# Leaving out the filler products in the first step of a recurrent attention and mixture-of-experts kernel on one Trainium2 core

## The chip, the core and the metric

The kernel runs on one core of a Trainium2 chip. A core has five engines with queues of their own: TensorE (PE in the profile, its weight loads PEld), VectorE (DVE), ScalarE (ACT), GpSimd (POOL) and SyncE (SP), which starts the transfers. Each executes its instructions in order and waits on semaphores that the others raise. The metric is the device time of the whole launch in microseconds (us).

## The reference, cut to what matters

The input x is (2, 2048, 256), 32-bit floats. It is normalised over its last axis and goes through two branches whose product is added back:

```
xn = layernorm(x)
dx = shift_by_one_token(xn) - xn
xm = xn + dx * x_miu
mix = tanh(xm @ x_A)                       # six groups of 32
miu = lambdas + mix[g] @ x_B[g]            # for r, w, k, v, a, g
r_in, w_in, k_in, v_in, a_in, g_in = xn + dx * miu
v = v_in @ vW.T;  r = r_in @ rW.T;  g = tanh(g_in @ g_A) @ g_B
w = -softplus(-(w_miu + tanh(w_in @ w_A) @ w_B)) - 0.5
k = normalised(k_in @ kW.T + tanh(k_in @ k_A) @ k_B)
a_gate = 2 * sigmoid(a_time + a_in @ a_A @ a_B)
y = wkv7(r, w, kk, v, -k, k * a_gate)      # recurrence over tokens, state 64x64 a head
s = (group_norm(y) + bonus) * g @ oW.T
f = sum over 8 experts of gate * (relu(xn @ wi.T + bi + lora_e) @ wo.T + bo)   # top 2
out = x + s * silu(f)
```

## The kernel before, in words

The 2048 tokens of both sequences are cut into 16 tiles of 2 x 64 tokens a sequence. A pipeline of three stages runs over them in 18 steps: "front" (norm, mixing, projections) of tile s in step s, "rec" (the recurrence and the experts) in step s + 1, "post" (the output product) in step s + 2. Step 1 holds a front alone. Each engine has a program written out by hand, in which the stages of a step are interleaved; inside an engine the order is fixed, and between engines semaphores set it.

In step 1 TensorE has little to do and waits often. Its order there is xt_ (four transposes of xn), route, mix (the product with x_A), miu(0), miu(1), kW, wk_A, g_A, wk_B, a_A, miu(2), a_B, norm, r_, v_, g_B, xmt_, bonus_, diag. What it waits for:

- route waits for ScalarE's xnc (the copy of the transposed xn out of PSUM, L911).
- mix waits for VectorE's xm (L1384).
- miu(0) waits for ScalarE's mixt, the tanh of mix's result (L919, L920), and for the second group of weight loads, of which w_kW is the last. ScalarE works on mixt after the exponentials of the expert gate (exps, L941 and L942).
- miu(1) waits for VectorE to have used miu(0)'s result (mtmp, L1394); GpSimd then adds xnc to it and makes xd (L1195), which kW, wk_A and the other projections read.
- r_ waits for the fifth xd; bonus_ for VectorE's dg (L1460).

Between these stand calls of warm, which multiplies one zeroed 128x128 block (the second xnc buffer, not yet used) with a zeroed 128x256 one into the bank FB; nobody reads the result. A call is two instructions on the chip, all with the line L297:

```
def warm(n):
    for _ in range(n):
        mm(FB[:, 0:256], xnc[1][:, 0, 0:128], xnc[1][:, 1, :], start=True, stop=True)
```

Step 1 has 21 calls: 5 before xt_, then 1, 2, 4 and 4 up to miu(1), 2 after norm and 3 after xmt_. The products of mm2, which most projections use, stand at L253 (in two halves of 64 columns) or L254 (whole).

Of the kernel before, what the change touches and what calls it, by code (L numbers as in the profile page):

```python
# [66 lines left out]
def program(nc, x, par, weights, consts, out):  # L67
    ctx = ExitStack()
    with ctx:
# [24 lines left out]
        def till(name, n):  # L94

            return S(name), at(name) + n
# [123 lines left out]
        def wait_loaded(engine, i):  # L220

            engine.wait_ge(loaded_by[i], 16 * (len(GROUPS[i]) + (i == 0)))
# [23 lines left out]
        def _(pe):  # L246
# [47 lines left out]
# [4 lines that stand above are left out]
# [19 lines left out]
            def xt_():  # L317
                pe.wait_ge(*till("xn_done", G))
                if not steps["front"]:
                    wait_loaded(pe, 0)  # L320
                to_channels(used_by("xt"), xn, "xt_mm")

            def route(half=False):
                pe.wait_ge(*till("xnc_done", 1))
                for g in range(G):
                    for c in range(2):
                        last = mm2(half, used_by("route")[:, g * 136:(g + 1) * 136], xnc[steps["front"] % 2][:, c, g * L:(g + 1) * L],
                                  w["route"][:, c, :], start=(c == 0), stop=(c == 1))
                last.then_inc(S("route_mm"), 1)

            def mix(half=False):
                pe.wait_ge(*till("xm_done", 2))
                for u in range(2):
                    for c in range(2):
                        last = mm2(half, used_by("mix")[:, u * 256:(u + 1) * 256], w["x_A"][:, c, u * 128:(u + 1) * 128], xm[:, c, :],
                                  start=(c == 0), stop=(c == 1))
                last.then_inc(S("mix_mm"), 1)

            def miu(pair):
                pe.wait_ge(*till("mixt_done", 2))  # L340
                for c in range(2):
                    for k in (2 * pair, 2 * pair + 1):
                        q = MIX_ORDER[k]
                        o, u = 32 * (q % 4), q // 4
                        last = mm(MIU[k % 2][:, c * 256:(c + 1) * 256],  # L345
                                  w["x_B"][o:o + 32, u, c * 128:(c + 1) * 128], mixt[o:o + 32, u, :], start=True, stop=True)
                last.then_inc(S("miu_mm"), 1)
# [7 lines left out]
            def wk_A():  # L355
                pe.wait_ge(*till(f"xd_{SLOT[W_]}_done", 1))
                pe.wait_ge(*till(f"xd_{SLOT[K_]}_done", 1))
                for c in range(2):
                    for o, name, q in ((0, "w_A", W_), (64, "k_A", K_)):
                        last = mm(used_by("wk_A")[o:o + 64, 0:G * L], w[name][:, c, :], xd[:, q, c, :], start=(c == 0), stop=(c == 1))  # L360
                last.then_inc(S("wk_A_mm"), 1)

            def a_A():
                pe.wait_ge(*till(f"xd_{SLOT[A_]}_done", 1))
                for c in range(2):
                    last = mm(used_by("a_A")[64 * c:64 * c + 64, 0:G * L], w["a_A"][:, c, :], xd[:, A_, c, :], start=True, stop=True)
                last.then_inc(S("a_A_mm"), 1)

            def g_A(half=False):
                low("g_A", G_, 128, half)  # L370

            def wk_B():
                pe.wait_ge(*till("hwk_done", 1))
                for c in range(2):
                    for o in (0, 64):
                        mm(used_by("wk_B")[o:o + 64, c * 256:(c + 1) * 256], w["wk_B"][0:64, c * 128 + o:c * 128 + o + 64],  # L376
                           h_wk[0:64, :], start=True, stop=True)
                        last = mm(used_by("kW")[o:o + 64, c * 256:(c + 1) * 256], w["wk_B"][64:128, c * 128 + o:c * 128 + o + 64],
                                  h_wk[64:128, :], start=False, stop=True, skip_group_check=True)
                last.then_inc(S("wk_B_mm"), 1)  # L380

            def a_B(half=False):
                pe.wait_ge(*till("ha_done", 1))
                for c in range(2):
                    last = mm2(half, used_by("a_B")[:, c * 256:(c + 1) * 256], w["a_B"][:, c * 128:(c + 1) * 128], h_a[:],
                              start=True, stop=True)
                last.then_inc(S("a_B_mm"), 1)

            def kW(half=False):
                pe.wait_ge(*till(f"xd_{SLOT[K_]}_done", 1))  # L390
                for c in range(2):
                    for k in range(2):
                        mm2(half, used_by("kW")[:, c * 256:(c + 1) * 256], w["kW"][:, k, c * 128:(c + 1) * 128], xd[:, K_, k, :],
                           start=(c == 0 and k == 0), stop=False, skip_group_check=True)

            def r_(half=False):
                pe.wait_ge(*till(f"xd_{SLOT[R_]}_done", 1))
                for c in range(2):
                    for k in range(2):
                        last = mm2(half, used_by("r")[:, c * 256:(c + 1) * 256], w["rW"][:, k, c * 128:(c + 1) * 128],  # L400
                                  xd[:, R_, k, :], start=(k == 0), stop=(k == 1))
                last.then_inc(S("r_mm"), 1)

            def v_(half=False):
                pe.wait_ge(*till(f"xd_{SLOT[V_]}_done", 1))
                for g in range(G):
                    for k in range(2):
                        last = mm2(half, used_by("v")[:, g * C:(g + 1) * C], xd[:, V_, k, g * L:(g + 1) * L], w["vW"][:, k, :],
                                  start=(k == 0), stop=(k == 1))
                last.then_inc(S("v_mm"), 1)  # L410
# [8 lines left out]
            def norm(half=False):  # L419
                pe.wait_ge(*till("ksum_done", 1))  # L420
                mm2(half, used_by("norm")[:, 0:G * L], ones[:], ksum[:], start=True, stop=True).then_inc(S("nrm_mm"), 1)
# [180 lines left out]
            def tile(step, front, rec, post):  # L602
# [13 lines left out]
                if step == 1:  # L616
                    if front:
                        xt_()
                        warm(1)
                        route()  # L620
                        warm(2)
                        mix()
                        warm(4)
                        if step == 1:
                            wait_loaded(pe, 1)
                        miu(0)
                        warm(4)
                        pe.wait_ge(*till("mx_0_done", 2))
                        pe.wait_ge(*till("mx_1_done", 2))
                        miu(1)  # L630
                        kW(half=True)
                        wk_A()
                        wait_loaded(pe, 2)
                        pe.wait_ge(*till("xnc_done", 1))
                        g_A(half=True)
                        pe.wait_ge(*till("route_read", 1))
                        wk_B()
                        pe.wait_ge(*till("mixt_done", 2))
                        a_A()
                        pe.wait_ge(*till("mx_2_done", 2))  # L640
                        pe.wait_ge(*till("mx_3_done", 2))
                        miu(2)
                        pe.wait_ge(*till("kraw_done", 1))
                        pe.wait_ge(*till("ksq_done", 1))
                        a_B()
                        pe.wait_ge(*till("hwk_done", 1))
                        norm()
                        warm(2)
                        pe.wait_ge(*till("hg_done", 1))
                        r_()  # L650
                        pe.wait_ge(*till("sig_done", 2))
                        v_()
                        pe.wait_ge(*till("ha_done", 1))
                        g_B()
                        pe.wait_ge(*till("agate_done", 2))
                        xmt_()
                        warm(3)
                        pe.wait_ge(*till("nrm_done", 1))
                        bonus_()
                        pe.wait_ge(*till("r_done", 1))  # L660
                        pe.wait_ge(*till("gate_done", 1))
                        diag(rec)
# [1230 lines left out]
```

## Time and profile before

| | us |
|---|---|
| median of 3 runs | 1017.18 |
| lowest and highest | 1015.92, 1017.49 |
| the profiled execution, as timed | 1017.24 |
| its span, first to last instruction | 1015.4 |
| TensorE busy | 997.9 |
| VectorE busy | 842.5 |
| ScalarE busy | 660.5 |

The profile shows one execution, in microseconds from its first instruction; what lies around the span is not in it. L297 is line 297 of the kernel. Matmuls overlap in the array: the start-to-start distance is less than the duration of one, and ends are modelled. The granted clock is TensorE's share of 2.4 GHz, so 1.00 is 2.4 GHz and 0.50 is 1.2 GHz.

### The profile page before, as it was taken

The page shows a single profiled execution, that of the slowest core. Times are in us where ns is not written, and L with a number is a line of the kernel's source. Part 1 is how long each engine was busy: PE and PEld are TensorE (multiplying, and loading weights), DVE is VectorE, ACT ScalarE, POOL GpSimd, SP SyncE. Part 2 cuts the span into 40 slices and gives each one's busy share as a digit, 9 for nine tenths or more (in the row PEclk, how much of TensorE's full clock was granted, in tenths as well). Part 3 has the DMA queues.
Part 4 walks back from the last instruction along what each step waited for, and adds up shares of the span by engine and source line. Part 5 has one row for each costly group of instructions (what it writes and reads, how often), then busy time and mean ns, then how long its engine had stood idle before and what let it go on. Part 6 is the DMA issues. An engine that isn't in the chain of part 4 may idle for free.

```text
span 1015.4 us, 45487 instructions
## 1 busy us (share of the span) xinstructions
PE 997.9 (98%) x19952; PEld 783.6 (77%) x19952; DVE 842.5 (83%) x1674; ACT 660.5 (65%) x1458; POOL 457.3 (45%) x541
## 2 busy tenths in 40 slices
PE   9999999999999999999999999999999999999996
PEld 6777778777787877778777787877778777787774
DVE  5887979888888888989888888888889889798864
ACT  3656675756768576676756767576676666757563
POOL 3372534535344362543635445363543725445422
PEclk9999999999999999999999999999999999999998
DMA  7000000000000000000000000000000000000000
GB/s 251 12 4 3 3 4 23 4 23 3 12 15 4 23 4 23 3 4 23 4 24 4 3 24 3 23 4 23 3 4 23 3 23 3 3 23 5 13 4 22
DMA packets 9267, 17.13 MB, mean 17 GB/s; under 512 B 1904, under 2 KB 3824, under 8 KB 8816
## 3 DMA queue, kind: packets, MB, share of 16 engines
q1 hardware_dynamic: 9072, 14.23, 4.3%
q8 instruction: 159, 2.61, 1.0%
q14 instruction: 36, 0.29, 0.1%
HBM read 10.03 MB, written 4.19 MB: 14 GB/s over the span
## 4 chain that ended last, share of the span: by engine, by line
PE 93%; DVE 3%; issue 2%; ACT 2%; POOLq 0%; POOL 0%; DVEq 0%
PE bank L254 37%; PE bank L253 14%; PE grams L468 10%; PE bank L345 5%; PE bank L494 2%; PE grams L537 2%; PE bank L483 2%; PE bank L527 2%; PE grams L442 2%; PE bank L568 2%; PE grams L592 2%; PE grams L557 2%; PE bank L360 2%; PE bank L376 2%; PE bank L302 2%
## 5 line engine op out<-in xcount | busy, mean ns | idle before, releaser
L1214 POOL TENSOR_TENSOR bk<-bk,tot 128x256 f32<-128x256 f32 x192 | 154.4, 815 | 209.2 <-PE grams L468 209.2
L1528 DVE COPY_PREDICATED gm<-c_mask_g,grams 128x1024 f32<-128x1024 int32 x96 | 160.1, 1668 | 13.9 <-PE grams L468 13.9
L900 ACT ACTIVATE relu<-bank,prm 128x256 f32<-128x256 f32 x256 | 107.1, 470 | 83.2 <-PE bank L254 82.0
L1195 POOL TENSOR_TENSOR xd<-mtmp,xnc 128x512 f32<-128x512 f32 x96 | 120.7, 1272 | 34.4 <-DVE mtmp L1394 34.4
L254 PE MATMUL bank<-xnc,w_wi 128*128 128x256 f32 x512 | 124.5, 386 | 0.4 <-ACT relu L900 0.4
L468 PEld LDWEIGHTS grams<-ar,bk 64*64 64x64 f32 x6144 | 100.3, 134 | 23.4 <-issue 15.3
L1004 ACT ACTIVATE gl<-gm 32x128 f32<-32x128 f32 x320 | 98.8, 309 | 28.3 <-DVE gm L1528 21.6
L254 PE MATMUL bank<-xmt,w_lora_B 128*128 128x256 f32 x444 | 114.5, 387 | 0.0
L468 PE MATMUL grams<-ar,bk 64*64 64x64 f32 x6144 | 111.4, 220 | 2.5 <-ACT scratch L1182 2.0
L254 PEld LDWEIGHTS bank<-xnc,w_wi 128*128 128x128 f32 x512 | 94.4, 190 | 18.3 <-issue 5.6
L1538 DVE TENSOR_TENSOR ar<-ar,tot 128x512 f32<-128x512 f32 x96 | 93.0, 968 | 17.5 <-PE grams L468 17.3
L1394 DVE SCALAR_TENSOR_TENSOR mtmp<-bank,prm,dx 128x256 f32<-128x256 f32 x192 | 80.2, 473 | 22.0 <-PE bank L345 22.0
L1245 POOL TENSOR_TENSOR bk<-kh,rootd 128x512 f32<-128x512 f32 x16 | 28.2, 1763 | 153.2 <-PE bank L527 150.0
L254 PEld LDWEIGHTS bank<-xmt,w_lora_B 128*128 128x128 f32 x444 | 80.5, 190 | 15.1 <-issue 5.0
L253 PE MATMUL bank<-w_wo,hid 128*64 128x256 f32 x768 | 90.9, 379 | 0.0
L253 PEld LDWEIGHTS bank<-w_wo,hid 128*64 128x64 f32 x768 | 52.6, 137 | 23.3
L1226 POOL TENSOR_TENSOR out_t<-out_t,x_in 128x512 f32<-128x512 f32 x16 | 20.3, 1268 | 77.0 <-DVE out_t L1517 77.0
L345 PE MATMUL bank<-mixt,w_x_B 32*128 32x256 f32 x384 | 54.3, 400 | 0.0
L1496 DVE TENSOR_TENSOR hid<-relu 128x512 f32<-128x512 f32 x64 | 48.4, 776 | 0.6
L911 ACT ACTIVATE xnc<-bank 128x512 f32<-128x512 f32 x15 | 9.0, 597 | 49.5 <-PE bank L302 49.5
L1577 DVE TENSOR_TENSOR state<-dec,bank 128x256 f32<-128x256 f32 x32 | 13.3, 417 | 33.2 <-PE bank L578 33.2
L1203 POOL TENSOR_TENSOR tot<-tot 128x256 f32<-128x256 f32 (+2 forms) x96 | 39.5, 412 | 2.7
(207 smaller groups left out, 2227.0 us busy)
## 6 DMA issues: line engine op xcount, KB each, us to landing
x_in<-x SPq DMA_DIRECT2D x16, 256.0 KB, 2.8
out<-out_t SPq DMA_DIRECT2D x16, 256.0 KB, 2.0
w_wi<-w_wi_dram SPq DMA_DIRECT2D x1, 1024.0 KB, 7.0
w_wo<-w_wo_dram SPq DMA_DIRECT2D x1, 1024.0 KB, 9.4
w_lora_B<-w_lora_B_dram SPq DMA_DIRECT2D x1, 512.0 KB, 8.8
w_x_A<-w_x_A_dram SPq DMA_DIRECT2D x1, 256.0 KB, 2.6
w_x_B<-w_x_B_dram SPq DMA_DIRECT2D x1, 256.0 KB, 2.6
w_kW<-w_kW_dram SPq DMA_DIRECT2D x1, 256.0 KB, 3.5
```

The lines of the kernel that those rows point to most:

```text
L253: last = mm(out[o:o + 64, :], lhsT[:, o:o + 64], rhs, **kw)
L254: return last if half else mm(out, lhsT, rhs, **kw)
L345: last = mm(MIU[k % 2][:, c * 256:(c + 1) * 256], w["x_B"][o:o + 32, u, c * 128:(c + 1) * 128], mixt[o:o + 32, u, :], start=True, stop=True)
L468: last = mm(dst, bk[o:o + 64, g, c, 1 - b, k, :], rhs, start=True, stop=True)
L900: A(dst[:, p % 2, j * 256:(j + 1) * 256], ZB[p % 2][:, j * 256:(j + 1) * 256], ACT.Relu, bias=prm[:, P_BI + 2 * p + j:P_BI + 2 * p + j + 1 ...
L1004: A(gl[l % 2][o:o + 32, :, :, :].rearrange("p q g (c n m) -> p (q g c) n m", c=2, m=m), right(gm[o:o + 32, :, :, :, b, 0, 32 * k:32 * k + ...
L1195: tt(xd[:, q, :, :], mtmp[:, k % 2, :, :], xnc[steps["front"] % 2][:, :, :], ALU.add).then_inc(S(f"xd_{k}_done"), 1)
L1214: tt(v, v, d, ALU.mult).then_inc(S(f"bk{k}_scaled"), 1)
L1394: run(v.scalar_tensor_tensor(mtmp[:, k % 2, c, :], MIU[k % 2][:, c * 256:(c + 1) * 256], prm[:, P_LAM + 2 * q + c:P_LAM + 2 * q + c + 1], ...
L1496: run(v.tensor_tensor(hid[:, p, :], relu1[:, p % 2, :], relu2[:, p % 2, :], ALU.add), f"hid_{p}_done")
L1528: run(v.copy_predicated(dst, msk.to_broadcast([128, 32, HALF // m, m]), src), "g_stored")
L1538: run(v.tensor_tensor(a, a, tv[:, :, 0].unsqueeze(1).unsqueeze(3).to_broadcast([128, 2, 4 * n, m]), ALU.mult), "ar_scaled")
```

## The change

Sixteen of the 21 calls of warm are left out: the 1, 2, 4 and 4 between xt_ and miu(1), the 2 after norm and the 3 after xmt_. The five before xt_ stay. No other instruction, wait or transfer is added, moved or taken away.

```
                     if front:
                         xt_()
-                        warm(1)
                         route()
-                        warm(2)
                         mix()
-                        warm(4)
                         if step == 1:
                             wait_loaded(pe, 1)
                         miu(0)
-                        warm(4)
                         pe.wait_ge(*till("mx_0_done", 2))
                         pe.wait_ge(*till("mx_1_done", 2))
                         miu(1)
...
                         norm()
-                        warm(2)
                         pe.wait_ge(*till("hg_done", 1))
                         r_()
...
                         xmt_()
-                        warm(3)
                         pe.wait_ge(*till("nrm_done", 1))
                         bonus_()
```

## Rows read from the trace of the kernel before

**Rows 1.** The page, the chain that ended last: shares by engine.

```profile
PE 93%; DVE 3%; issue 2%; ACT 2%; POOLq 0%; POOL 0%; DVEq 0%
```

**Rows 2.** Timeline of TensorE, 0 to 18 us: start, duration, instructions, [idle before].

```profile
1.99 4.63 PE L297 MATMUL bank<-xnc 128*128 128x256 f32 x10 [1.99 <-DVE scratch L1786]
...
7.50 0.66 PE L297 MATMUL bank<-xnc 128*128 128x256 f32 x2
8.39 1.19 PE L254 MATMUL bank<-w_route,xnc 128*128 128x136 f32 x8 [0.24 <-ACT xnc L911]
9.42 1.03 PE L297 MATMUL bank<-xnc 128*128 128x256 f32 x4
10.28 1.89 PE L254 MATMUL grams<-xm,w_x_A 128*128 128x256 f32 x8
12.01 1.89 PE L297 MATMUL bank<-xnc 128*128 128x256 f32 x8
13.83 1.13 PE L345 MATMUL bank<-mixt,w_x_B 32*128 32x256 f32 x8
14.89 1.99 PE L297 MATMUL bank<-xnc 128*128 128x256 f32 x8
16.82 1.13 PE L345 MATMUL bank<-mixt,w_x_B 32*128 32x256 f32 x8
```

**Rows 3.** Timeline of all engines, 0 to 18 us: VectorE and ScalarE.

```profile
9.24 0.88 DVE L1384 SCALAR_TENSOR_TENSOR xm<-dx,prm,xnc 128x256 f32<-128x256 f32 x2
...
11.91 0.28 ACT L942 ACTIVATE e<-top,nm 128x1 f32<-128x1 f32 x1
12.21 0.38 ACT L919 ACTIVATE mixt<-grams 128x256 f32<-128x256 f32 x1
12.49 0.36 ACT L920 ACTIVATE mixt<-grams 64x256 f32<-64x256 f32 x1
...
15.01 1.66 DVE L1394 SCALAR_TENSOR_TENSOR mtmp<-bank,prm,dx 128x256 f32<-128x256 f32 x4 [4.31 <-PE bank L345]
```

**Rows 4.** The chain that ended last, 14 to 37 us: start, length, piece.

```profile
22.65 0.60 ACT kraw L959
...
33.06 0.48 DVE dg L1460
```

**Rows 5.** Timeline of TensorE, 27 to 34 us.

```profile
27.09 1.97 PE L254 MATMUL grams<-xd,w_rW 128*128 128x256 f32 x8 [0.51 <-POOL xd L1195]
...
33.68 0.43 PE L449 MATMUL bank<-dg,c_headsel 128*32 128x128 f32 x8 [0.30 <-DVE dg L1460]
```

**Rows 6.** Single lines: durations in ns (min/median/max), first and last start.

```profile
L297 PE MATMUL bank<-xnc x6: 631/631/792, 2.0 to 4.3; 128*128 128x256 f32 x6
...
L297 PE MATMUL bank<-xnc x42: 379/379/792, 2.0 to 33.0; 128*128 128x256 f32 x42
...
L302 PE MATMUL grams<-c_ident,xn x4: 421/421/444, 6.6 to 7.3; 128*128 128x128 f32 x4
...
L302 PE MATMUL bank<-c_ident,xn x4: 272/272/273, 42.0 to 42.4; 128*128 128x128 f32 x4
```

**Rows 7.** Windows: length, TensorE busy (instructions), granted clock, DMA share, GB/s.

```profile
954.80:956.80 2.00, 0.00 (x0) 1.00 0.00 0
...
1001.25:1004.25 3.00, 0.00 (x1) 1.00 0.21 81
1004.25:1004.75 0.50, 0.00 (x0) 0.55 0.00 0
1007.20:1010.90 3.70, 3.67 (x16) 0.50 0.00 0
...
1011.00:1011.25 0.25, 0.00 (x0) 0.75 0.00 0
```

**Rows 8.** A weight load: its issue in the timeline, and KB and us to landing.

```profile
6.38 0.44 SPq L1800 DMA_DIRECT2D w_kW<-w_kW_dram x1
...
w_kW<-w_kW_dram SPq DMA_DIRECT2D x1, 256.0 KB, 3.5
```

More of the change, by code:

```diff
@@ L618, in tile @@
                         xt_()
-                        warm(1)
                         route()
-                        warm(2)
                         mix()
-                        warm(4)
                         if step == 1:
@@ L626, in tile @@
                         miu(0)
-                        warm(4)
                         pe.wait_ge(*till("mx_0_done", 2))
@@ L647, in tile @@
                         norm()
-                        warm(2)
                         pe.wait_ge(*till("hg_done", 1))
@@ L656, in tile @@
                         xmt_()
-                        warm(3)
                         pe.wait_ge(*till("nrm_done", 1))
```

## The prediction

> **What bounds the kernel now.** I read the page first: TensorE carries 93% of the chain that ended last [rows 1]. So whatever delays TensorE in the first step delays the end by as much, unless another engine was the later one at that place. The change touches only the first 35 us, so I read the timeline of TensorE there [rows 2], beside it what ScalarE and VectorE did when TensorE waited [rows 3], then the chain for the places where it leaves TensorE [rows 4], the two late groups of fillers [rows 5], the durations that tell the clock at the start [rows 6], the windows in which the granted clock fell and rose later [rows 7], and a weight load [rows 8].
>
> The reader is to see three things. First, TensorE looks busy from 1.99 to 25 us, but the rows L297 are fillers: products of a zeroed buffer that nobody reads. Second, behind each group of fillers stands a real group that waits for another engine, so a filler costs something only where it ends later than that engine. Third, the first five fillers (10 instructions) ran at half the later speed.
>
> **The unit.** One call of warm is two matmul instructions (10 for warm(5) in [rows 2]). At the full clock the eight instructions of mix take 1.89 us [rows 2], the last of them 0.38 to its modelled end, as the median product of this width does [rows 6]: (1.89 - 0.38)/7 = 0.216 us from start to start, so 0.43 us a call. The change removes 16 calls, 32 instructions: 32 x 0.216 = 6.9 us of TensorE's time. Nearly all of it lies in waits.
>
> **The change, group by group.**
>
> - warm(1) at 7.50: two instructions, gone by about 8.0. route starts at 8.39, released by ScalarE's xnc, with 0.24 us idle before it [rows 2]. Worth 0.
> - warm(2) at 9.42: four instructions, 9.42 + 0.86 = 10.28, where mix starts. VectorE's xm ends at 9.24 + 0.88 = 10.12 [rows 3]. How long TensorE takes from a release to its start I read at two places where it had run out of work: miu(1) starts at 16.82 after VectorE's 15.01 + 1.66 = 16.67, 0.15 later [rows 2, 3]; bonus starts at 33.68 after 33.06 + 0.48 = 33.54, 0.14 later [rows 4, 5]. By 0.15 mix would start at 10.27. Even with no delay at all (10.12) it wins nothing: the product goes to ScalarE's mixt, which starts at 12.21 behind the last exponential, ended at 11.91 + 0.28 = 12.19 [rows 3]. Worth 0.
> - warm(4) at 12.01: eight instructions, 12.01 + 1.73 = 13.74; miu(0) starts at 13.83. What miu(0) needs, mixt, is ready at 12.49 + 0.36 = 12.85 [rows 3]. The last of the loads that it waits for, w_kW, was issued at 6.38 and took 3.5 [rows 8], so it is in by 9.9 to 10.3 and does not hold it. Without fillers it starts at 12.85 + 0.15 = 13.00: **0.83 us earlier**. The bounds are 0.98 (no delay from the release) and 0.6 (the 0.36 that the last ScalarE instruction itself takes as a delay, as a pessimistic one). This is the one group on the path.
> - warm(4) at 14.89: 14.89 + 1.73 = 16.62, and VectorE, which miu(1) waits for, ends at 16.67 [rows 2, 3]. The two end together: 0 to 0.10 to gain; I take 0.05.
> - warm(2) before r_: r_ starts at 27.09 after 0.51 us in which TensorE idled for GpSimd's xd, fillers done [rows 5]. Worth 0, with 0.5 us of slack.
> - warm(3) before bonus: bonus starts at 33.68, after 0.30 us idle for VectorE's dg, which ends at 33.54 [rows 4, 5]. Worth 0, 0.3 us of slack.
>
> **Does the 0.88 reach the end?** Up to 22.6 us the chain is TensorE alone: miu(1), kW, wk_A, g_A, wk_B follow each other, and wk_B's end releases ScalarE's kraw at 22.65 [rows 4]. Each input of these (xd from GpSimd) descends from miu(0) and moves with it. From 22.65 to 33.54 the chain is ScalarE and VectorE (two table loads, square root, reciprocal, kh, dg), again from wk_B's end, so it moves too; bonus and diag follow it and step 2 follows them with no pause. Nothing with a time of its own stands in between: the weight loads that step 1 waits for landed before they were wanted, and no engine gets another instruction or wait. So the sum is 0.83 + 0.05 = 0.88, about **0.9 us**, against 1017.24 us for the profiled execution (span 1015.4 and 1.8 around it): **1016.3**. The median of the three runs shown, 1017.18, is the same time, but the three spread over 1.6 us.
>
> **The clock, which can take it back.** The granted clock is the only other thing the fillers touch. The windows call it 1.00 from time 0, but durations say otherwise: the first fillers took 631 ns against 379 ns later, and the transposes at 6.6 to 7.3 took 421 ns against 272 ns at 42 us [rows 6]. So TensorE was at 1.2 GHz until about 7.5 us, after 5.6 us of work, and at 2.4 GHz for route. The five fillers that stay, and the transposes behind them, are what ran before the rise; the first removed filler begins only at 7.50.
>
> After the change TensorE pauses four times: about 0.5 us before route, 0.8 before mix, 0.9 before miu(0) (12.1 to 13.0), 1.8 before miu(1) (14.1 to 15.9), then works densely to 25; later some 1.5 us each before r_ and before bonus. Later in the trace a single pause of 2.0 us at 954.80 left the clock at 1.00; one from 1001.25 had let it fall in the window 1004.25 to 1004.75, after 3.0 us or more; and it came back in 1011.00 to 1011.25, just after 3.7 us of dense work at 0.50 [rows 7]. Every pause of the changed kernel is shorter than the one that did no harm. But no row shows several with only 1.1 us of work between two of them, as here around miu(0), and clock changes need not meet the program at the same place in each execution.
>
> The price if it falls: dense work of 3.7 to 3.9 us at half speed before it rises, as at 1007.2, is work that takes half as long at the full clock: a loss of **1.9 us** per fall. Where the work at half speed has slack behind it, less.
>
> The Trainium skill (TensorE: Matmul & The Clock Gate, section "A second HAM failure mode: psum-queue depth-cycling") says that frequent short idles between groups of matmuls can make the clock swing between its levels. That rule speaks against this change; the trace neither bears it out nor excludes it, for before the change it has no such row of pauses. By it the result would be the second or third rival below rather than the forecast.
>
> **Rivals.**
>
> 1. *Nothing comes of it.* Another release turns out as late as the filler (a delay of 0.9 us at miu(0)). Against it: 0.15 and 0.14 measured at two such places. Time: 1017.2.
> 2. *The clock falls once*, in the pauses around miu(0) (12.1 to 15.9), and miu(1), kW and wk_A run at half speed until it returns. For it: two pauses close together, 2.7 us idle out of 3.8. Against it: the 2.0 us pause that did nothing. Time: 1016.3 + 1.9 = 1018.2. With a second fall before bonus, so that step 2 begins slow: 1020.1.
> 3. *The five fillers alone don't carry the clock up* and it stays low through the thin stretch. Extra, doubling what is on the path: route's issue doubles and ends near 10.3, mix then takes 7 x 0.43 + 0.63 = 3.6 us to 13.9, mixt's two instructions 0.64 (12.21 to 12.85) and the release 0.15, so miu(0) is late by 14.7 - 13.0 = 1.7 us; if work at half speed raises the clock there, it ends at 1016.3 + 1.7 = 1018.0. If it holds on through both miu (2 x 0.9) and the first 3.8 us of the dense stretch (1.9), the sum is 1016.3 + 1.7 + 1.8 + 1.9 = **1021.7**. This is the one that ends on the other side. It decides as soon as the slow work costs 2.9 us (0.9 given back and 2.0 on top), that is once miu(1) too runs slow. For it: the rise came only at about 7.5, at the edge of what stays. Against it: at half speed route and mix close up by themselves to over 5 us of nearly unbroken work, more than preceded the rise at 1011.
>
> **How the numbers follow.** A run of this kernel tells no change from one below 0.2%, about 2.0 us. Forecast (clock stays, 0.9 us gained): 0.58, at 1016.3. Rival 1: 0.07. Rival 2 with one fall: 0.16, at 1018.2. Rival 3 with an early rise: 0.05, at 1018.0. These four are all within 0.2%, 0.86 less some 0.04 for noise in either direction: 0.82. Slower: rival 3 in full (0.08), two falls (0.04), and 0.02 of that noise: 0.14. Faster: the other 0.02 of the noise and 0.02 for what I have not seen, 0.04; the terms found sum to 0.9 us, and even their upper bounds (0.98 + 0.10) to 1.1. The low end of the range is the fastest run shown less the gain, 1015.92 - 0.9 = 1015.0; the high end, 1019.2, is one fall (1018.2) and 1.0 more for the spread of the runs. It leaves out two falls and rival 3 in full.
>
> **What would show it.** miu(0) at 13.0 instead of 13.83, mixt unmoved at 12.21; miu(1) at 15.9 to 16.0; kraw at 21.8; bonus at 32.8; 379 ns for every 256-column product after 8.4 us, and idle time before miu(1) of some 1.8 us. A kW or miu(1) product of some 630 ns means rival 2; route products of twice 279 ns mean rival 3. The prediction is wrong if the clock falls for more than one short stretch, or if step 2 does not move with bonus.

## The result and the profile after

The changed kernel takes 1020.48 us (median of 13 runs, 1018.49 to 1022.82), the kernel before 1017.18 (13 runs, 1015.92 to 1018.58). The ratio is 1.003, with a 95% interval from 1.0022 to 1.0039: **slower by 3.3 us**, where 0.9 us faster was forecast and 1019.2 was the top of the range. The granted clock says where to look. Its mean over a run is 0.989 to 0.993 in the 13 runs of the changed kernel (median 0.991), and 0.993 to 0.998 in the 86 runs of the kernel before that stand beside the experiments below (median 0.996); only five of these 86 have 0.993.

The profiled execution of the changed kernel is its shortest: 1018.49 us, span 1016.7. This is its timeline of TensorE in the first step, to be held against [rows 2, 5]; line numbers of VectorE and ScalarE are 6 lower than before.

```profile
6.34 0.63 PE L302 MATMUL grams<-c_ident,xn 128*128 128x128 f32 x4 [0.29 <-DMA c_eye<-c_eye_dram]
7.66 1.19 PE L254 MATMUL bank<-w_route,xnc 128*128 128x136 f32 x8 [0.69 <-ACT xnc L905]
9.44 1.99 PE L254 MATMUL grams<-xm,w_x_A 128*128 128x256 f32 x8 [0.59 <-DVE xm L1378]
12.26 1.13 PE L345 MATMUL bank<-mixt,w_x_B 32*128 32x256 f32 x8 [0.83 <-ACT mixt L914]
15.15 1.70 PE L345 MATMUL bank<-mixt,w_x_B 32*128 32x256 f32 x8 [1.75 <-DVE mtmp L1388]
16.78 3.02 PE L253 MATMUL bank<-xd,w_kW 128*64 128x256 f32 x16
...
26.61 1.96 PE L254 MATMUL grams<-xd,w_rW 128*128 128x256 f32 x8 [0.92 <-POOL xd L1189]
...
33.64 0.42 PE L449 MATMUL bank<-dg,c_headsel 128*32 128x128 f32 x8 [2.04 <-DVE dg L1454]
```

What ends the waits before miu(0) and miu(1), from the timelines of ScalarE and VectorE:

```profile
11.75 0.36 ACT L914 ACTIVATE mixt<-grams 64x256 f32<-64x256 f32 x1
```

```profile
13.43 1.66 DVE L1388 SCALAR_TENSOR_TENSOR mtmp<-bank,prm,dx 128x256 f32<-128x256 f32 x4 [3.46 <-PE bank L345]
```

The forecast gain is there. Before, miu(0) started 13.83 - 12.85 = 0.98 us after mixt was ready; now it starts 12.26 - 12.11 = 0.15 after, so 0.83 us are won, exactly the term of the sum. Before miu(1) the distance fell from 0.15 to 15.15 - 15.09 = 0.06, 0.09 won where 0.05 was put. Together 0.92.

(That mixt itself is ready 0.74 us earlier than before is no effect of the change, for the transposes stand ahead of all that was left out. They began 0.28 us earlier (6.34 against 6.62) and took 0.63 in place of 1.08 us, at the full clock already, as they did too when the kernel before was run again.)

Then the loss. miu(1) takes 1.70 us where it took 1.13, and the 16 halves of kW take 3.02 us where they took 1.95. kW in the kernel before:

```profile
17.88 1.95 PE L253 MATMUL bank<-xd,w_kW 128*64 128x256 f32 x16
```

The windows of the profile after (length, busy time of PE, PEld, DVE, ACT, POOL, granted clock, DMA share, GB/s):

```profile
12.00:15.00 3.00, 1.13 (x8) 0.76 (x8) 1.57 (x4) 0.11 (x1) 0.61 (x1) 1.00 1.01 300
15.00:16.00 1.00, 0.85 (x6) 0.75 (x8) 0.09 (x1) 0.00 (x0) 1.00 (x2) 0.79 1.00 328
16.00:18.50 2.50, 2.50 (x12) 1.14 (x12) 1.61 (x5) 0.00 (x0) 1.52 (x2) 0.50 1.00 395
18.50:19.50 1.00, 1.00 (x10) 0.62 (x8) 0.90 (x5) 0.00 (x0) 1.00 (x2) 0.76 1.09 457
...
958.00:961.00 3.00, 3.00 (x18) 2.34 (x12) 2.71 (x2) 0.00 (x0) 2.59 (x5) 0.50 0.00 0
```

The clock falls between 15 and 16 us, just as miu(1) begins, and is back between 18.5 and 19.5. From mixt to bonus it is 33.64 - 12.11 = 21.53 us, before 33.68 - 12.85 = 20.83. So 0.70 slower although 0.92 were won: this fall cost 1.6 us. A second stretch at half speed lies at 958, behind the pause before step 17, which the change does not touch; the kernel before kept 1.00 there, up to 1004 us. What it costs shows further below, where the time is taken apart.

### The profile page after: what moved, and what is told of

Same layout as the page of the kernel before. It is cut to its first block, busy times and chain, and to the rows that moved or that the text cites. A ratio compares the mean times of both kernels' runs of the same rounds, so it can differ in the third digit from the quotient of the medians.

```text
span 1016.7 us, 45423 instructions
## 1 busy us (share of the span) xinstructions
PE 993.4 (98%) x19920; PEld 779.3 (77%) x19920; DVE 842.0 (83%) x1674; ACT 660.4 (65%) x1458; POOL 456.9 (45%) x541
## 4 chain that ended last, share of the span: by engine, by line
PE 89%; DVE 6%; issue 2%; ACT 2%; SPq 0%; DMA 0%; POOLq 0%; POOL 0%; DVEq 0%
PE bank L254 36%; PE bank L253 13%; PE grams L468 10%; PE bank L345 5%; PE grams L537 2%; PE bank L494 2%; PE bank L483 2%; PE bank L527 2%; PE grams L442 2%; PE bank L568 2%; PE grams L592 2%; PE grams L557 2%; PE bank L360 2%; PE bank L376 2%; DVE gm L1522 2%
```

## The experiments

Each median below is to be held against the kernel before, run in turn with it on the same chip: 1017.15 us for the first four (35 runs), 1017.05 for the others (22 and 29 runs on two other chips). Only the fillers differ between these kernels; none changes what is computed for the output.

**The kernel before, again** (no edit).

> The kernel before, unchanged, to see the mean granted clock of its runs beside their times. If the difference is the clock, its runs have 0.995 to 0.996 (one stretch at the end at half speed, and the last 3 us) against 0.989 to 0.993 for the changed kernel, and the time is 1017.2. If the changed kernel loses elsewhere, its clocks are as low as those of the changed kernel.

1016.96 us, ratio 0.9998 (0.999 to 1.0007), clocks 0.995 to 0.998. Its profile holds 1.00 from the rise to the pause of the last step:

```profile
6.60:1003.00 996.40, 987.45 (x19923) 777.28 (x19922) 837.86 (x1655) 656.00 (x1450) 451.88 (x528) 1.00 0.05 16
```

So the lower clocks belong to the change.

**The early groups back, the late ones out.**

```
                         xt_()
+                        warm(1)
                         route()
+                        warm(2)
                         mix()
+                        warm(4)
...
                         miu(0)
+                        warm(4)
```

> The changed kernel with the four groups up to miu(1) (1, 2, 4 and 4 calls) back, the two late groups (2 and 3) still out. Theory A (the clock falls in the pauses around miu(0) and miu(1), or does not rise before them): 1017.0 to 1017.5, clock 0.995. Theory B (the clock falls in the two late pauses, before r_ and bonus, and step 2 begins slow): 1019.5 to 1020.5, as the changed kernel. If both pauses count: between, 1018 to 1019.

1018.26 us, ratio 1.0009 (0.9999 to 1.0018): 1.1 us over the kernel before, 2.2 under the changed one. Its runs have clocks of 0.993 to 0.998. The interval of the ratio just includes no loss at all, but it ends below that of the changed kernel, which begins at 1.0022: putting the early groups back helps, and they are the larger part. By the medians it is the case between, in which both pauses count.

**The late groups back, the early ones out.**

```
                         norm()
+                        warm(2)
...
                         xmt_()
+                        warm(3)
```

> The changed kernel with the two late groups (2 calls after norm, 3 after xmt_) back, the four early ones out. Theory A: still 1020 to 1020.5. Theory B: 1016.3, with the 0.9 us that the early groups give back. Both: 1018 to 1019.

1019.30 us, ratio 1.0021 (1.0012 to 1.0029): 2.15 over the kernel before, 1.2 under the changed one. The two parts add up by the medians, 1.1 + 2.15 = 3.25 against 3.3, though the 1.2 won here lies within the noise (the changed kernel's interval is 1.0022 to 1.0039). Theory B would have given 1016.3 and has fallen as the sole cause. The profile has the fall at 15 to 16 us again, and none behind the late pause:

```profile
15.00:16.00 1.00, 0.74 (x6) 0.64 (x8) 0.20 (x1) 0.00 (x0) 1.00 (x2) 0.84 1.08 369
16.00:18.80 2.80, 2.80 (x16) 1.39 (x14) 1.75 (x6) 0.00 (x0) 1.81 (x2) 0.50 1.03 415
...
33.00:40.00 7.00, 6.02 (x152) 4.99 (x152) 5.06 (x14) 2.90 (x8) 0.85 (x3) 1.00 0.01 2
```

**Only the group between miu(0) and miu(1) back.**

```
                         miu(0)
+                        warm(4)
```

> The changed kernel with only the group between miu(0) and miu(1) (4 calls) back. Theory A in the form that the 1.8 us pause before miu(1) makes the clock fall: if it is the only cause, 1016.3 and a clock of 0.995. Theory C (the five first fillers alone often leave the clock low, and it rises late): little better than the changed kernel, 1019 to 1020. Theory B: no better than the changed kernel.

1019.25 us, ratio 1.0019 (1.001 to 1.0028). I had expected 1016.3 if that pause was the only cause. The time would fit theory C, but the profile does not: the clock was up before route, as in all the others. In its profile it does cure the fall at 15 us; the first fall now comes behind the late pause, where this kernel has no filler:

```profile
14.00:18.00 4.00, 4.00 (x30) 2.68 (x30) 2.66 (x8) 0.00 (x0) 2.99 (x3) 1.00 0.94 352
30.00:33.00 3.00, 1.18 (x19) 0.69 (x21) 2.90 (x5) 2.71 (x6) 1.60 (x2) 1.00 0.00 0
33.40:34.00 0.60, 0.60 (x42) 0.60 (x35) 0.28 (x2) 0.24 (x2) 0.00 (x0) 0.63 0.00 0
34.00:36.80 2.80, 2.80 (x21) 2.23 (x14) 2.19 (x6) 0.20 (x1) 0.19 (x1) 0.50 0.02 6
```

**The changed kernel, a second and a third profile** (no edit).

> The changed kernel, unchanged, for a second profile of it. By the mean clocks of its 13 runs (0.989 to 0.993) the theory of the clock expects four or five stretches of 3.4 us at half speed, against two in the kernel before: one or more in the first 20 us, where TensorE pauses before miu(0) and miu(1), perhaps one at 33 to 40 us behind the pause before bonus, the two at the end. If the loss is elsewhere, 1.00 from 6 to 1000 us and a step longer than 61.35.

> The changed kernel unchanged, for a third profile. The theory of the clock expects a stretch at half speed that begins at 15 to 16 us, behind the pause before miu(1), as in both profiles of it so far, and the time to follow the number of such stretches: 1.7 us for each over the two of the kernel before, less 0.9.

1023.93 and 1020.52 us, one execution each; the first is longer than all 13 runs above. The second profile shows all the places at once. Its windows:

```profile
15.00:16.00 1.00, 0.68 (x4) 0.60 (x6) 0.27 (x1) 0.00 (x0) 1.00 (x2) 0.69 0.93 336
16.00:22.00 6.00, 6.00 (x30) 3.23 (x28) 4.34 (x14) 0.00 (x0) 3.53 (x3) 0.50 1.01 400
22.00:23.00 1.00, 1.00 (x11) 0.65 (x8) 0.83 (x6) 0.38 (x1) 0.00 (x0) 0.89 1.06 323
...
35.40:36.40 1.00, 0.67 (x17) 0.46 (x20) 1.00 (x2) 0.98 (x3) 0.00 (x0) 0.73 0.00 0
36.40:39.20 2.80, 2.80 (x67) 2.50 (x64) 1.55 (x4) 0.06 (x1) 0.00 (x0) 0.50 0.00 0
```

Here the clock stays low twice as long after miu(1), and falls again as step 2 begins. In its timelines mixt is ready at 12.29 and bonus starts at 35.49: 23.20 us, against 20.83 before, so 2.4 more, or 3.3 for the fall with the 0.92 won taken out. The mark that ScalarE leaves at the end of step 2 tells what the second fall costs, and the one at the end of step 16, which releases TensorE into step 17, what comes later. In the order before, after, second and third profile of the changed kernel, each from its own timeline:

```profile
97.05 0.20 ACT L1182 ACTIVATE scratch<-eps 128x1 f32<-128x1 f32 x1
...
956.55 0.19 ACT L1182 ACTIVATE scratch<-eps 128x1 f32<-128x1 f32 x1
```

```profile
97.02 0.20 ACT L1176 ACTIVATE scratch<-eps 128x1 f32<-128x1 f32 x1
...
956.61 0.20 ACT L1176 ACTIVATE scratch<-eps 128x1 f32<-128x1 f32 x1
```

```profile
100.24 0.20 ACT L1176 ACTIVATE scratch<-eps 128x1 f32<-128x1 f32 x1
...
960.54 0.19 ACT L1176 ACTIVATE scratch<-eps 128x1 f32<-128x1 f32 x1
```

```profile
98.87 0.20 ACT L1176 ACTIVATE scratch<-eps 128x1 f32<-128x1 f32 x1
...
958.79 0.19 ACT L1176 ACTIVATE scratch<-eps 128x1 f32<-128x1 f32 x1
```

With mixt ready at 12.85, 12.11, 12.29 and 12.50, bonus at 33.68, 33.64, 35.49 and 34.08, and the ends of the spans, each execution falls into four parts:

| us | before | after | second | third |
|---|---|---|---|---|
| mixt ready to bonus | 20.83 | 21.53 | 23.20 | 21.58 |
| to the end of step 2 | 63.37 | 63.38 | 64.75 | 64.79 |
| to the end of step 16 | 859.50 | 859.59 | 860.30 | 859.92 |
| to the end of the span | 58.85 | 60.09 | 61.56 | 59.91 |

The two executions whose clock fell at 34 to 36 lose 1.4 us in the second part, the other none. In the last part all three lose 1.1 to 2.7 us, and all three have a stretch at half speed as step 17 begins, which the kernel before has not. In the profile after, that is nearly the whole difference of the two spans: 1016.7 - 1015.4 = 1.3 us, of which 1.24 arise there.

In the third profile the first fall comes after 17 us, not at 15 to 16 as I had expected, and takes part of kW and wk_A instead of miu(1); and its time is not 1.7 us for each stretch less 0.9. Its stretches at 17, 34 and 959 us would give 5.1 - 0.9 = 4.2 over the kernel before; it has 3.5, for the second and the third cost less (1.42 and 1.06 in the table).

**Fillers of 16 columns.** The kernel before with all its calls, but narrow ones after the first five. This tells array work from the mere presence of the instructions.

```
-mm(FB[:, 0:256], xnc[1][:, 0, 0:128], xnc[1][:, 1, :], ...)
+mm(FB[:, 0:256 if n == 5 else 16], xnc[1][:, 0, 0:128],
+   xnc[1][:, 1, 0:256 if n == 5 else 16], ...)
```

> The kernel before, with the 16 later fillers still there as instructions, but 16 columns wide in place of 256, so that they take almost no time in the array; the first five are left as they were. Theory A (what the fillers give is array work that holds the clock up): as the changed kernel, 1019.5 to 1020.5, mean clock 0.991 to 0.993. Rival (their instructions or order matter, such as the weight loads or the place where TensorE stands at its waits): as the kernel before, 1017.2 and 0.996.

1019.11 us, ratio 1.0023 (1.0011 to 1.0035), clocks 0.989 to 0.994: 0.4 under the range expected for theory A, but its interval overlaps that of the changed kernel and lies clear of the kernel before. The fillers between miu(0) and miu(1) are there, and miu(1) runs slow all the same:

```profile
13.56 1.07 PE L297 MATMUL bank<-xnc 128*128 128x16 f32 x8
15.38 1.89 PE L345 MATMUL bank<-mixt,w_x_B 32*128 32x256 f32 x8 [0.76 <-DVE mtmp L1394]
```

**Fillers fitted to the waits.**

```
 xt_(); warm(1); route(); warm(2); mix()
-warm(4)
+warm(2)
 miu(0); warm(4); ...
 norm()
-warm(2)
+warm(3)
 ...; xmt_(); warm(3); bonus_()
```

> Fillers fitted to the waits: 1, 2, then 2 calls in place of 4 before miu(0) (they end at 12.87, when mixt is ready), 4 before miu(1), 3 in place of 2 before r_, 3 before bonus. The theory of two separate terms (0.8 us of delay at miu(0), the rest clock) expects the 0.8 us without the loss: 1016.3, mean clock 0.996 as before. If every gain in step 1 ends in a longer wait for VectorE: 1017.1.

1016.94 us, ratio 0.9993 (0.9984 to 1.0002), clocks 0.994 to 0.998. In its profile mixt is ready at 12.02 + 0.36 = 12.38 and miu(0) starts at 12.53, 0.15 later, as in the changed kernel, with no fall until the end. The time is 0.1 us under that of the kernel before by the medians and 0.7 by the ratio; the interval holds both no gain and all of the expected 0.8.

**Three groups, only for the long pauses.**

```
                         miu(0)
+                        warm(4)
...
                         norm()
+                        warm(3)
...
                         xmt_()
+                        warm(3)
```

> The changed kernel with three groups back: 4 calls between miu(0) and miu(1), 3 before r_, 3 before bonus; nothing between the transposes and miu(0). If the three long pauses (1.8, 1.0 and 2.0 us) are what lets the clock fall: 1016.3 to 1017, mean clock 0.996. If the short pauses before route, mix and miu(0) count too: 1018 to 1019.

1016.84 us, ratio 0.9996 (0.9987 to 1.0004). It lies in the range expected for the three long pauses. The fillers between the transposes and miu(0) are not needed: their pauses may stay if the long ones are filled.

**Fillers in the last steps too.** f1, and calls before step 17, before the last transposes and before the output product, the last two into a bank whose reader is done (warm takes the bank as a second argument for that).

```
                         v_()
+                        if step == TILES:
+                            pe.wait_ge(*till("y1_read", 1)); warm(4)
...
                         rec_inc(1)              # end of step 17
+                        pe.wait_ge(*till("relu2_3_done", 2)); warm(7, ZB[1])
...
                         zt_()
+                        if step == TILES + 2: warm(3, ZB[1])
```

> f1, and fillers in the pauses of the last steps: 4 calls in the 2.0 us before step 17, 7 in the 3.5 us before the last transposes, 3 before the output product. If the clock is what these pauses cost, the stretch at half speed at 1004 to 1011 disappears: transposes 1.08 to 0.60, output product 3.68 to 1.90 us, so 2.2 us less than f1, and 0.5 more on average from the pause before step 17: 1013.6, mean clock 0.999 or more. Rival (the end hangs on VectorE, ScalarE and the store, not on TensorE): no change against f1.

1014.42 us, ratio 0.9972 (0.9962 to 0.9983): 2.6 us under the kernel before, the fastest version of the study. The end of its timeline, and below it that of f1:

```profile
1000.80 3.29 PE L297 MATMUL bank<-xnc 128*128 128x256 f32 x14
1004.40 0.63 PE L302 MATMUL bank<-c_ident,zz 128*128 128x128 f32 x4 [0.31 <-DVE scratch L1787]
1004.87 1.46 PE L297 MATMUL bank<-xnc 128*128 128x256 f32 x6
1006.85 1.95 PE L253 MATMUL bank<-w_oW,zt 128*64 128x256 f32 x16 [0.52 <-ACT zt L995]
```

```profile
1003.87 1.08 PE L302 MATMUL bank<-c_ident,zz 128*128 128x128 f32 x4 [3.53 <-DVE scratch L1780]
1006.31 3.60 PE L253 MATMUL bank<-w_oW,zt 128*64 128x256 f32 x16 [1.36 <-ACT zt L988]
```

The output product takes 1.95 instead of 3.60 us: 1.65 us at the end of the path. The transposes take 0.63 instead of 1.08, but that gives nothing. The output product waits for ScalarE's zt, and zt stands behind a table load and ysg, here in f1:

```profile
1003.85 1.28 ACT L992 ACT_TABLE_LOAD   x1
1005.14 0.63 ACT L992 ACTIVATE ysg<-y 128x512 f32<-128x512 f32 x1
1005.68 0.58 ACT L988 ACTIVATE zt<-bank 128x512 f32<-128x512 f32 x1
```

So the output product starts 2.45 us after the transposes start (1006.85 - 1004.40), where it was 2.44. I had counted both terms, and f2 ends 0.8 us above the expected 1013.6. The medians of f1 and f2 differ by 2.5 us. The other 0.9 may be what falls before step 17 cost in some runs of f1, but the two profiles can't show it: the clock fell there in neither.

**The changed kernel with those end fillers, and with the one before step 17 alone** (the edits of f2 on the changed kernel, all three and the first only).

> The changed kernel (early and late groups of step 1 out) with the fillers of f2 in the last steps: 4 before step 17, 7 before the last transposes, 3 before the output product. If the change costs its 3.3 us only in and behind step 1 (theory A and B together), it is as far above f2 (1014.4) as the changed kernel above the kernel before: 1017.7, mean clock 0.995 to 0.997. If part of the loss arises in the pauses of the last steps, because the early change moves them against the clock: less, 1016 to 1016.5.

> The changed kernel with only the 4 calls before step 17. The clock fell behind that pause in all five profiles of kernels without the early or the late fillers (957 to 961 us) and in none of three with them. If that is more than chance and part of the 3.3 us, this wins 1.2 to 1.7 us against the changed kernel: 1018.8 to 1019.3. If it falls there in every kernel equally often, it wins about 0.5: 1020.

All three: 1017.45 us, ratio 1.001 (1.0 to 1.002), 3.0 above f2. f2 has the early start of miu(0) too, so this is to be held against the distance of the changed kernel from f1, 1020.48 - 1016.94 = 3.5: most of the loss stands when the end is covered, as expected if it arises in steps 1 and 2.

Its twelve runs also show how the time follows the clock. With a mean of 0.998 they take 1015.7 to 1016.3 us (three runs, among them the profiled one, whose only stretch at half speed is that at 15 us), with 0.996 or 0.997 1017.3 to 1018.7 (five), with 0.995 1019.2 to 1020.9 (four); the seven of f2 have 0.999 to 1.000 and take 1013.7 to 1015.2. By the windows of the profile after, a stretch at 15 to 19 us takes 0.21 + 1.25 + 0.24 = 1.7 us of granted clock, 0.0017 of the mean. So, as an estimate, these runs had one, two and three such stretches, at 1.5 to 2.3 us each by the means of the groups, and the typical run had two.

The filler before step 17 alone: 1018.85 us, ratio 1.0026 (1.0015 to 1.0036), against 1.003 (1.0022 to 1.0039) without it. The medians favour a gain of 1.6 us; the intervals overlap, so it stays undecided.

**All profiles together.** These counts go by the granted clock of the 14 profiles. Where the pauses around miu(0) and miu(1) had no full-width filler, the clock fell between 15 and 17.2 us in seven profiles of seven (the changed kernel three times, e2, e5, g1, g2). Where at least the one before miu(1) was filled, it fell there in none of seven. Behind the late pause it fell in four of eight profiles without wide fillers (a1, a2, e3, e5) and in none of six with them. Behind the pause before step 17, where that has no filler, it fell in seven of eleven: in the changed kernel's three, e2, e3, e5 and j1, not in the kernel before (twice), e1 and f1. From the end of step 16 to the last product of step 17 (L578) it is 45.1 to 46.8 us in these seven and 43.7 to 44.4 in the four, 1.6 more on average. The seven are just the profiles without full-width fillers between the transposes and miu(0), the four those with them. But the mean clocks of the runs do not bear that out: those of j1 (0.993 to 0.996, median 0.996) are no lower than those of f1 (0.994 to 0.998, median 0.995).

## Why the prediction was wrong

- *Which filler delays anything*: right. Only the one before miu(0) did, 0.83 us by forecast and by the profile; with miu(1) 0.92 against 0.88.
- *That this moves on to the end*: the chain moved with miu(0) as described up to the point where the clock fell. By itself the gain can't be told from the noise in the kernels that keep the clock (f1, j1).
- *The clock stays*: **this step failed.** It rested on "Every pause of the changed kernel is shorter than the one that did no harm". The single pause of 2.0 us was no measure for 0.8 and 1.8 us with 1.1 us of miu(0) between them: six falls in six profiles with these pauses bare, and one in one with the narrow fillers in them. Nor was it safe itself, since the clock falls behind just that pause in seven of eleven executions; one profile that had kept it was taken for a rule. The rival of one fall (1018.2) was described at its place, with a chance of 0.16, and that of two (1020.1), next to which the median of 1020.48 came out, with 0.04. Together they should have had nearly all.
- *The price of a fall*, put at 1.9 us: 1.6 in the profile after, 3.3 in the second profile, where the clock stayed low twice as long, 1.4 for the late one, 1.2 for the one behind step 17 in the profile after. The size was about right; what was missing was that it may stay down longer, and that several places fall in one execution.
- *The late pauses*, taken as some 1.5 us each: right where the clock had held up to there (1.38 before r_ and 1.58 before bonus in e1 and e3). In the changed kernel, behind the slow stretch, they are 0.92 and 2.04. The late groups, which I priced at nothing, cost 1.1 us by e1's median when left out, with an interval that reaches down to nothing.
- *Rival 3*, the five fillers alone don't carry the clock up: wrong in every profile; route ran at 279 ns in all those of the changed kernel.
- *The rule of the Trainium skill* (TensorE: Matmul & The Clock Gate, "A second HAM failure mode: psum-queue depth-cycling"), that frequent short idles between groups make the clock swing: the runs agree with it, 1.00 to 0.50 and back within 4 to 8 us, and it deserved more weight than the one row against it.
- *The sum, and what is open*: -0.9 for the early start and 3.0 for the falls in steps 1 and 2 (g1 against f2) make 2.1 us. With 1.2 for the fall behind step 17, as in the profile after, it is the 3.3 between the medians. But whether that fall comes more often because of the change is not settled: the three profiles of the changed kernel against the two of the kernel before and g2's median speak for it, while g1 against f2, and the changed kernel against f1, leave only 0.5 us for it. What decides whether the clock falls behind a given pause, when it does in four of eight or seven of eleven, no run here shows.

## What to carry to other kernels

A filler has two prices: the delay of what stands behind it, read from the release and the start of the next real group, and what the clock does to the dense work that follows the pause. Fit it to the wait so that it ends as the release comes; here that delayed nothing and the clock held. And look for pauses (1.6 to 3.5 us here), or several close together, ahead of dense work anywhere in the kernel, the last steps included: there fillers won 2.5 us here.

## What was not expected of the hardware

Eight fillers of 16 columns did not hold the clock, though the profile of that kernel shows TensorE busy in the window for 2.60 of 3.00 us, against 1.13 in the changed kernel:

```profile
12.00:15.00 3.00, 2.60 (x21) 2.10 (x20) 1.33 (x4) 0.35 (x2) 0.38 (x1) 1.00 1.04 329
15.00:16.00 1.00, 0.62 (x4) 0.54 (x6) 0.33 (x1) 0.00 (x0) 1.00 (x2) 0.81 0.91 336
```

So the busy time on a page does not tell whether the clock will hold. And the fall is not at once: the work before miu(1) was thin, but the clock was still 1.00 through 12 to 15 us and fell when the dense work had begun.
